# A relational graph layer: summing neighbours after the projection instead of before it, with the opening of the kernel reordered

## The reference

```python
x = x + _L0_gnn_ref(_layernorm(x), edge_index, edge_type_3, query_embs, W_rel1, W_root1, b1, ...)

def _rgcn(x, W_rel, W_root, bias, src, dst, etype):
    xr = jnp.einsum('ni,rio->rno', x, W_rel)
    msg = xr[etype, src]
    out = x @ W_root + bias
    for r in range(3):
        m = etype == r
        s = segment_sum(jnp.where(m[:, None], msg, 0.0), dst, num_segments=n)
        c = segment_sum(m, dst, num_segments=n)
        out = out + s / jnp.maximum(c, 1.0)[:, None]
    return out

def _gate(h, q, Wg, bg, Wq, bq):            # 8 groups: 32 rows of h and 64 query rows each
    hg = h3 @ Wg[:, :F].T                   # "node rows"
    qg = q @ Wg[:, F:].T + bg               # "query rows"
    attn = sigmoid(hg[:, :, None, :] + qg[:, None, :, :])
    qi = einsum('bnlf,blf->bnf', attn, q)
    alpha = sigmoid(h3 @ Wq[:, :F].T + qi @ Wq[:, F:].T + bq)
    return alpha * tanh(qi) + (1.0 - alpha) * h3

h = relu(_rgcn(x, W_rel1, W_root1, b1, ...)); h = _gate(h, ...)
h = relu(_rgcn(h, W_rel2, W_root2, b2, ...)); h = _gate(h, ...)
```

## Time and profile before

| what | value |
|---|---|
| median of 3 runs | 2180.86 us (2179.66 to 2183.28) |
| the profiled execution | 2177.92 us, span 2175.9 us |
| PE busy | 1935.8 us (89%) |
| DVE, ACT, POOL busy | 33%, 20%, 14% |
| chain that ended last | PE 64%, DMA 13%, DVE 12%, POOL 7% |

### The profile page before, as it was taken

The page is one execution under the profiler, slowest core; times in us unless marked ns, Lnnn a source line. Parts: engine busy times, 40 slices in busy tenths (PEclk is TensorE's granted clock), DMA queues, the critical chain, the costliest instruction groups (busy, mean ns, idle before and its releaser), DMA issues.

```text
span 2175.9 us, 22184 instructions
## 1 busy us (share of the span) xinstructions
PE 1935.8 (89%) x9644; PEld 1241.9 (57%) x9644; DVE 717.7 (33%) x1195; ACT 443.9 (20%) x811; POOL 311.5 (14%) x181
## 2 busy tenths in 40 slices
PE   5799998999988999997988988888899798989999
PEld 2487444874436888866755433333455544757876
DVE  3611999218995111125043000000422222032110
ACT  0001555005552010014041000000421000031110
POOL 0000888007881000000010000000000000010000
PEclk9999999999998999996988999999999899999999
DMA  7320300313002555550212999999733244202550
GB/s 293 87 87 18 135 1 1 139 44 145 1 0 89 218 221 220 234 224 1 102 44 89 429 428 428 430 428 428 305 155 151 99 194 198 83 22 114 196 196 16
DMA packets 33892, 363.98 MB, mean 167 GB/s; under 512 B 6813, under 2 KB 10149, under 8 KB 11898
## 3 DMA queue, kind: packets, MB, share of 16 engines
q1 hardware_dynamic: 28906, 357.03, 40.8%
q10 hardware_dynamic: 4880, 5.43, 1.0%
HBM read 356.93 MB, written 0.79 MB: 164 GB/s over the span
## 4 chain that ended last, share of the span: by engine, by line
PE 64%; DMA 13%; DVE 12%; POOL 7%; ACT 2%; issue 1%; SPq 0%; ACTq 0%; DVEq 0%
PE banks L112 61%; POOL gate_work L118 7%; DMA weight_ring<-in_L_ffn_c_fc_dram 6%; DVE gate_work L118 5%; DMA weight_ring<-in_L_ffn_c_proj_e_dram 4%; PE banks L115 3%; DVE gate_qiT L132 2%; DMA weight_ring<-in_L_gnn_W_in_dram 1%; DVE stat L243 1%; DMA A_sd<-in_c_selg_dram 1%; ACT at_P L146 1%; DVE stat L132 0%; SPq L152 0%; DVE att_P L129 0%; DVE xn_tok L123 0%
## 5 line engine op out<-in xcount | busy, mean ns | idle before, releaser
L118 POOL TENSOR_TENSOR gate_work<-gate_work 128x1024 f32<-128x1024 f32 x144 | 284.7, 1990 | 268.7 <-DVE gate_work L118 264.9
L112 PE MATMUL banks<-gate_sel,gate_rows 96*128 96x512 bf16 x1152 | 279.9, 381 | 29.5 <-DVE gate_work L118 29.3
L118 DVE TENSOR_TENSOR gate_work<-banks,gate_qT 128x1024 f32<-128x1024 f32 x192 | 226.2, 1220 | 13.4 <-ACT banks L146 3.8
L146 ACT ACTIVATE banks<-banks 128x1024 f32<-128x1024 f32 x192 | 193.3, 1008 | 132.9 <-PE banks L112 132.9
L112 PEld LDWEIGHTS banks<-gate_sel,gate_rows 96*128 96x128 bf16 x1152 | 105.0, 97 | 182.3 <-DVE gate_work L118 74.9
L112 PEld LDWEIGHTS banks<-r_xd,weight_ring 128*128 128x128 f32 x1728 | 197.5, 192 | 9.0 <-issue 1.6
L112 PE MATMUL banks<-r_xd,weight_ring 128*128 128x128 f32 x1728 | 197.9, 275 | 1.0 <-issue 1.0
L112 PE MATMUL banks<-weight_ring,xT 128*128 128x384 f32 x576 | 193.2, 492 | 5.0 <-DVE rgat_xr L135 1.5
L118 POOL TENSOR_TENSOR stat<-stat 128x1 f32<-128x1 f32 (+1 forms) x23 | 14.6, 633 | 1239.0 <-DVE stat L122 1104.5
L112 PE MATMUL banks<-xT,weight_ring 128*128 128x256 f32 x792 | 187.0, 389 | 5.0 <-ACT x_tok L149 1.6
L112 PEld LDWEIGHTS banks<-xT,weight_ring 128*128 128x128 f32 x792 | 154.3, 196 | 33.8 <-issue 2.3
(11 more groups left out here) (330 smaller groups left out, 1847.5 us busy)
## 6 DMA issues: line engine op xcount, KB each, us to landing
weight_ring<-in_L_ffn_c_fc_dram SPq DMA_DIRECT2D x32, 2304.0 KB, 23.2
weight_ring<-in_L_ffn_c_proj_e_dram SPq DMA_DIRECT2D x32, 2304.0 KB, 23.3
weight_ring<-in_L_ffn_w_gate_dram SPq DMA_DIRECT2D x8, 2304.0 KB, 12.7
weight_ring<-in_L_ffn_w_up_dram SPq DMA_DIRECT2D x8, 2304.0 KB, 9.2
weight_ring<-in_L_ffn_w_down_dram SPq DMA_DIRECT2D x8, 2304.0 KB, 8.7
weight_ring<-in_L_ffn_w_dram SPq DMA_DIRECT2D x16, 1152.0 KB, 7.8
weight_ring<-in_L_gnn_W_dram SPq DMA_DIRECT2D x7, 2304.0 KB, 13.7
weight_ring<-in_L_gnn_W_rel_dram SPq DMA_DIRECT2D x6, 2304.0 KB, 16.2
```

The lines of the kernel that those rows point to most:

```text
L112: return self.e.matmul(out, lhsT, rhs, start=start, stop=stop)
L118: return self.e.tensor_tensor(out, a, b, op)
L146: return self.e.activation(out, a, f, **kw)
```

## The change

In both graph layers the order of the two products is turned round: first each relation's projection of the rows, `xw[r]` = x times `W_rel[r]` (24 matmuls of 384 columns into four banks, copied out by ACT), then for all relations the neighbour sums over `xw[r]`, 36 matmuls of 256 columns on top of the root projection, now in banks 0 to 2 (first layer) or 4 to 6 (second). `aggT`, its DVE copies and the turning back after the first gate are gone. Relu starts with each finished pair of chunks.

In the opening, `x` comes first and is normed first; the relations' weights follow it on SP, and all other constants move to ACT's queue. The first layer's 36 projection steps of two matmuls stand one behind each edge chunk. The counts are summed by DVE along the free dimension of `A_ds` before the transposes, for which `in_degree` and `A_mean` are new. The eight query units move behind the first graph layer. The one-hot rows and tables lie in `gate_rows`. `step_bank` and `hidden_bank` use the banks in another order.

```diff
+        xw = [buf.rearrange("p (c n) -> p c n", c=TC) for buf in (xn_flat, flat[:, 0:2 * D], flat[:, 2 * D:4 * D])]
...
+        in_degree = stat[:, 40:40 + TC * NREL]
...
         def start_sp(q):
-            for dst, src in ((ident[:], dram["c_ident"]), (selrow[:], dram["c_selrow"]), (desc[:], dram["c_desc"]),
-                             (iota_slot[:], dram["c_iota_slot"]), (before[:], dram["c_before"]),
-                             (x_tok[:], dram["x"])):
-                q.dma(dst, src).then_inc(*mark("consts", 0, 16))
-            smalls_dma(q, "L0_ffn")
-            q.dma(iota, dram["c_iota"]).then_inc(*mark("edges", 0, 16))
-            for i, n in enumerate(("src", "dst", "edge_type_3")):
-                q.dma(eidx[:, i, :], dram[n]).then_inc(*mark("edges", 0, 16))
+            for dst, src in ((x_tok[:], dram["x"]), (ident[:], dram["c_ident"])):
+                q.dma(dst, src).then_inc(*mark("x_in", 0, 16))
+            rgcn_sp(q, 0)
             load(q, "Wgq", dram["L0_gnn_Wg"][1])
             q.dma(qT[:], dram["L0_gnn_query_T"]).then_inc(*mark("gate_in", 0, 16))
+
+        def start_dma_act(a):
+            a.dma(iota, dram["c_iota"]).then_inc(*mark("edges", 0, 16))
+            for i, n in enumerate(("src", "dst", "edge_type_3")):
+                a.dma(eidx[:, i, :], dram[n]).then_inc(*mark("edges", 0, 16))
+            a.dma(sel_f, dram["c_selg"]).then_inc(*mark("sel_in", 0, 16))
             for i, n in enumerate(("L0_gnn_b1", "L0_gnn_b2", "L0_gnn_bq")):
-                q.dma(bcol[:, i, :], dram[n]).then_inc(*mark("gate_in", 0, 16))
-            q.dma(brow[:], dram["L0_gnn_bg"]).then_inc(*mark("gate_in", 0, 16))
-            q.dma(sel_f[:, 0:SELN], dram["c_selg"][:, 0:SELN]).then_inc(*mark("sel_in", 0, 16))
-            q.wait_ge(*at("sel_cast", 0))
-            q.dma(sel_f[:, 0:SELN], dram["c_selg"][:, SELN:2 * SELN]).then_inc(*mark("sel_in", 1, 16))
-
-        def start_act(a):
-            a.wait_ge(*at("consts"))
-            for n in range(NQ):
-                query_split_act(a, n)
-
-        def start_pool(g):
-            g.wait_ge(*at("consts"))
+                a.dma(bcol[:, i, :], dram[n]).then_inc(*mark("gate_in", 0, 16))
+            a.dma(brow[:], dram["L0_gnn_bg"]).then_inc(*mark("gate_in", 0, 16))
+            for dst, src in ((selrow[:], dram["c_selrow"]), (desc[:], dram["c_desc"]),
+                             (iota_slot[:], dram["c_iota_slot"]), (before[:], dram["c_before"])):
+                a.dma(dst, src).then_inc(*mark("consts", 0, 16))
+            smalls_dma(a, "L0_ffn")
...
+            v.e.memset(ones[:], 1.0)
+            v.wait_ge(*at("x_in"))
+            norm_dve(v, "L0_gnn", as_tok(xn_tok[:]), as_tok(x_tok[:]), 1e-5)
+            tok_to_T_dve(v, "L0_gnn")
...
-                if k % 4 == 3 and k >= 7:
-                    query_split_dve(v, k // 4 - 1)
...
+            v.wait_ge(*at("A_ds"))
+            by_rel = A_ds[:].rearrange("p c r s -> p (c r) s")
+            v.then(v.red(in_degree, by_rel, ALU.add))
+            v.then(v.ts(in_degree, in_degree, 1.0, ALU.max))
+            v.then(v.rec(in_degree, in_degree))
+            v.tt(A_mean.rearrange("p c r s -> p (c r) s"), by_rel, bc(in_degree.unsqueeze(2), [P, TC * NREL, T]),
+                 ALU.mult).then_inc(*mark("A_mean"))
             for r in range(NREL):
                 v.wait_ge(*at("A_turned", r))
-                v.cp(A_sd[:, r, :, :].rearrange("p k t -> p (k t)"), PS[:, r, :]).then_inc(*mark("A_sd_raw", r))
+                v.cp(A_sd[:, r, :, :].rearrange("p k t -> p (k t)"), PS[:, 3 + r, :]).then_inc(*mark("A_sd", r))
+            for n in range(NQ):
+                query_split_dve(v, n)
...
+        def start_xw_pe(pe, n):
+            r, n = divmod(n, TC * DC)
+            c, k = divmod(n, DC)
+            if n == 0:
+                pe.wait_ge(*loaded(("rel", 0, r)))
+            if k == 0 and r:
+                pe.wait_ge(*at("xw", (0, r - 1, c)))
+            for h in range(2):
+                t = xw_step_pe(pe, 0, r, c, k, h)
+            if k == DC - 1:
+                t.then_inc(*(mark("unit_free", ("rel", 0, r)) if c else mark("xw_ps", r)))
+
+        def xw_act(a, l, r, c):
+            b = xw_bank(l, r) + 2 * c
+            a.wait_ge(*(at("xw_ps", r) if l == 0 and c == 0 else at("unit_free", ("rel", l, r))))
+            a.copy(xw[r][:, c, :].rearrange("p (h n) -> p h n", h=2), PS[:, b:b + 2, 0:HALF]).then_inc(*mark("xw", (l, r, c)))
+
+        def start_pe(pe):
+            pe.wait_ge(*at("x_in"))
+            tok_to_T_pe(pe, "L0_gnn", "L0_gnn")
+            wait_T(pe, "L0_gnn")
+            for k in range(EC):
+                edges_pe(pe, k)
+                start_xw_pe(pe, k)
+            for n in range(EC, NREL * TC * DC):
+                start_xw_pe(pe, n)
+            pe.wait_ge(*at("A_ds"))
+            root_pe(pe, 0, range(4))
+            pe.wait_ge(*at("A_mean"))
             for r in range(NREL):
...
+                if r == 1:
+                    pe.wait_ge(*at("xw", (0, 2, 0)))
+                    pe.wait_ge(*at("xw", (0, 2, 1)))
...
+                        t = pe.tr(PS[:, 3 + r, k * T + c * P:k * T + c * P + P], A_mean[:, c, r, k * P:(k + 1) * P])
                 t.then_inc(*mark("A_turned", r))
...
+            root_pe(pe, 0, range(4, DC))
+            agg_pe(pe, 0)
+            query_pe(pe)
...
         def rgcn_sp(q, l):
-            load(q, ("root", l), dram[f"L0_gnn_W_root{l + 1}"])
             for r in range(NREL):
                 load(q, ("rel", l, r), dram[f"L0_gnn_W_rel{l + 1}"][r])
...
+        def agg_pe(pe, l):
             for o in range(DC):
+                for r in range(NREL):
+                    if o == 0:
+                        if l == 0:
+                            pe.wait_ge(*at("A_sd", r))
+                        for c in range(TC):
+                            pe.wait_ge(*at("xw", (l, r, c)))
+                    for k in range(TC):
+                        t = pe.mm(PS[:, acc_bank(l, o), o % 2 * T:(o % 2 + 1) * T], xw[r][:, k, o * P:(o + 1) * P],
+                                  A_sd[:, r, k, :], False, o % 2 == 1 and r == NREL - 1 and k == TC - 1)
+                if o % 2:
+                    t.then_inc(*mark("agg", (l, o // 2)))
+
...
+        def second_rgcn_pe(pe):
+            for r in range(NREL):
+                pe.wait_ge(*loaded(("rel", 1, r)))
+                if r == 2:
+                    for c in range(TC):
+                        pe.wait_ge(*at("xw", (1, 0, c)))
...
-            for r in range(NREL):
-                for f in range(DC):
-                    step = r * DC + f
-                    if step >= 2:
-                        pe.wait_ge(*at("agg_sb", (l, step - 2)))
-                    for k in range(TC):
-                        t = pe.mm(PS[:, 6 + step % 2, 0:T], h_tok[:, k, f * P:(f + 1) * P], A_sd[:, r, k, :], k == 0,
-                                  k == TC - 1)
-                    t.then_inc(*mark("agg", (l, step)))
-                pe.wait_ge(*at("agg_sb", (l, r * DC + DC - 1)))
-                project_T_pe(pe, ("rel", l, r), aggT, False, r == NREL - 1)
-
...
+                    if r == 0 and k % 2 == 0:
+                        pe.wait_ge(*at("gated", (0, k // 2)))
+                    for c in range(TC):
+                        for h in range(2):
+                            t = xw_step_pe(pe, 1, r, c, k, h)
+                t.then_inc(*mark("unit_free", ("rel", 1, r)))
+            for c in range(TC):
+                pe.wait_ge(*at("xw", (1, 1, c)))
+            root_pe(pe, 1, range(DC))
+            agg_pe(pe, 1)
...
-        def step_bank(step):
-            return 2 * ((step + 2) % 3)
-
-        def hidden_bank(c):
-            return 2 if c else 6
+        def hidden_bank(l, c):
+            return 2 * (c if l else 1 - c)
+
+        def step_bank(l, step):
+            return hidden_bank(l, step % 3 - 1) if step % 3 else 4
...
+            start_dma_act(a)
+            tok_to_T_act(a, "L0_gnn")
+            for r in range(2):
+                for c in range(TC):
+                    xw_act(a, 0, r, c)
+            a.wait_ge(*at("sel_in"))
+            a.copy(selg[:], sel_f).then_inc(*mark("sel_cast"))
+            for c in range(TC):
+                xw_act(a, 0, 2, c)
```

204 lines of the change are left out of this document (82 added, 122 removed).

## The result

| | before | changed |
|---|---|---|
| median | 2180.26 us, 4 runs (2179.32 to 2183.28) | 2149.60 us, 4 runs (2144.56 to 2152.34) |
| profiled execution, its span | 2177.92, 2175.9 | 2150.89, 2149.1 |
| POOL's first fold, first gate | 218.45 | 195.18 |
| POOL's first fold, second gate | 497.75 | 468.05 |

The ratio is 0.9854, 95% interval 0.9833 to 0.9876: 1.5% faster, 31 us. Forecast were 2144 and a range of 2135 to 2156. The first fold, forecast for 187.2, came 8.0 us later than that.

What follows compares the result with a forecast made beforehand. PE's work being unchanged, the gain must come from idle time in the opening and waits: 31.2 us at the first gate plus 5.4 in the second layer, 36.6 off 2180.86, gives 2144 us, range 2135 to 2156.

Steps and rivals of the forecast that it cites:

- work on PE starts: Opening: PE's work counts as starting at 14.8 us, first relation's weights there at 15.5, one 0.7 us chunk before.
- query rows' DMAs: Before the first gate: six DMAs exposed behind the last split, 11.8 us, bounds 10.1 and 13.4.
- -2 to +3: Opening: allowance in us for the start within the forecast's own range, 2138 to 2152.
- rival (a): Opening later: `x` lands at 8.1, weights at 20 or more, 6 to 8 us lost, 2151 us; chance 0.13.
- first chunk at 5.8 + 6.65 + 1.5 = 14.0: Opening: `x` landing 5.8, first statistics to first product with `xT` 6.65, cast of edge lists to first count 1.5.
- ACT's fifteen DMA issues, about 7 us: Opening: costed at nothing, as done before ACT's first copy, which waits for transposes at 9.4 or later.
- Rival (b): Shorter waits: query rows in 10.1 us, no slow beginning, weights at 13; 2138 us; chance 0.12.
- the 2.1 that would have refuted it: First layer: forecast is wrong if a step of chunk and projections takes more than 2.1 us.
- rival (c): First layer: projections amid the chunks don't fit, 0.7 us lost per step, 25 us, time 2169; chance 0.05.
- rival (d): Opening: PE held at 1.2 GHz, its 70 us take twice as long, 2214 us; chance 0.02.
- 0 to +3: First gate: allowance in us for a slow clock after PE's new idle, within the forecast's own range.
- Everything after the second gate I take as shifted whole: Rest of program: follows from when the second gate ends, same steps, shifted by 36 to 37 us.

Runs made afterwards that it cites:

- experiment 1: Changed kernel with edge loads on SP: 2136.24 us; ACT's last six issues late: 2150.71; both: 2138.17; SP's later weights held until edge lists land: 2135.45.
- experiment 3: Changed kernel with the first layer's projections all behind the 34 counting chunks instead of amid them: 2155.97 us, one run.
- experiment 2: Changed kernel with query rows sent by SP in quarters as splits finish, not by ACT behind the last split: 2144.91 us, ratio 0.9821.
- experiment 4: Kernel before with only the second layer's change: 2183.00, again 2181.16 us; changed kernel with second layer as before: 2158.84; changed again: 2149.07; before again: 2182.89.

## Why the prediction was right, and where its terms were not

**The mechanism held:** the idle time between PE's first count and the node rows went (18.8 us), and the gates start earlier, by 23.3 and 29.7 us where 31.2 and 36.6 were forecast. No run separates the two parts of the change in the first layer. Its own stretch before, 113.80 to 195.69, had only 2.2 us of idle; so, by the rows, the new order of the products helps there because projections don't need the adjacency and can fill its waits. The terms, in the profiled execution:

| term | forecast | measured | off |
|---|---|---|---|
| work on PE starts | 14.8 | 22.75 | +8.0 |
| from there to the node rows | 144.5 | 142.0 | -2.5 |
| to the last split | 2.4 | 2.5 | +0.1 |
| query rows' DMAs | 11.8 | 12.9 | +1.1 |
| ACT's first cast to POOL's first fold | 13.7 | 15.1 | +1.4 |
| first fold | 187.2 | 195.2 | +8.0 |
| between the two first folds | 273.9 | 272.9 | -1.0 |
| behind the second | 1678.2 | 1681.0 | +2.9 |

Sum: +9.9, and 0.2 less outside the span: the execution took 2150.89, not 2141.3, +9.6. It lies 1.3 above its median, where before's lay 2.9 below, so the median is off by 5.6 only. Those 4 us are luck. The first fold at 195.2 lies 8.0 behind the forecast, and the start alone exceeds the "-2 to +3" that the forecast's own range allowed it. The total stays inside the wider range, whose upper end was set for rival (a).

**The start** is the mis-sized term. The step that failed is "first chunk at 5.8 + 6.65 + 1.5 = 14.0". The 1.5 from the cast to the first count is right (13.33 to 14.82 with the weights held), and the 6.65 is (6.77 to 13.33 there); DVE began at 6.8 to 7.1 and not at 5.8: `x` landed at 6.1, but `x_in` counts the identity too, which landed at 7.0. But nothing in the sum asked when the edge lists land. With the weights held the first count came at 14.82, which agrees with the forecast 14.8 by luck: 0.8 of that was to be a wait for the first relation's weights, and no such wait showed; the 0.8 came from `x` and the identity. I reckoned ACT's loads only as bytes that could delay the weights, 12.3 to 16.6. The reverse happened: the weights delayed ACT's small loads. "ACT's fifteen DMA issues, about 7 us" cost at nothing was wrong as well, 20 us and not 7: in the changed kernel it held PE 1.4 us longer than the edge lists did, and taken away alone it gained nothing (experiment 1). That the start scatters by 2 us (22.75 and 23.62 in the changed kernel, 24.42, 24.82 and 24.84 in three with the same opening) was not in the sum either. Rival (a), 2151, has the right size by the wrong way: `x` landed before DVE's 7.06 and not at 8.1, and PE's first projection at 23.98 didn't wait for weights. Rival (b) fails by its query rows, 12.9 and not 10.1, and by the slow beginning, which was there.

**The stretch on PE**, term by term: chunks and projections 70.4 with the slow beginning in it (71.9 forecast), root product and transposes 10.4 and 1.3, the rest 5.2, neighbour sums 15.6, query units 39.1 (38.5; 4.91 each and not 4.81), handovers none (1.0), all from start to start. A step took 1.94 (30.40 to 32.34), under the 2.1 that would have refuted it; rival (c) is refuted by that and by experiment 3, rival (d) by the granted clock, 1.00 from 26.5 us, where its record begins, to the node rows, and by the first step at the full pace, at 26.52.

**The query rows** lay within their bounds, 10.1 to 13.4, and PE's idle of 7.12 within the 4 to 8 announced. What I priced too low is what that idle brings: the earlier trace rows showed that transposes after 13.36 us of idle take nearly twice as long, and I gave the first sums after the new idle no such term in the 13.7, only "0 to +3" in the range. The group was 5.28 - 2.75 = 2.5 us longer, and 1.1 of that reached the first fold. Without the idle, in experiment 2, the term is 189.53 - 175.81 (ACT's first cast there) = 13.7, as forecast.

**The second layer** gained 6.4 by the folds, 5.4 forecast, its best bound 6: from 369.18 to 446.77 the work took 77.6 us and not 78.8, and between two groups on PE there was no handover that can be seen. The kernel before took 279.3 and 281.0 between its folds in two executions, so a tenth of this is not to be read. "Everything after the second gate I take as shifted whole" is right for the instructions and wrong for the time, by 2.9 us here and by up to 10.6 in experiment 4. That is larger than most terms I worked out to a tenth.
